# Latent attention with three-pass fp32r scores and a division after the context, written out without loops

## The chip, the cores and the metric

One core of one Trainium2 chip runs a whole model of two blocks in one program. The metric is device time in microseconds (us), the median over several executions. The names of the engines are those of the profile: PE is the TensorE matmul, PEld its weight load, DVE is VectorE, ACT is ScalarE, POOL is GpSimd, SP issues the DMAs.

## The reference

The input is 1024 tokens of 256 channels. Eight residual layers follow each other: an attention, an expert layer (64 experts), a second attention, the expert layer again, a third attention, a small feed-forward, a **latent attention**, and the small feed-forward again. The change is in the latent attention alone:

```python
bs, seq_len, _ = x.shape                       # 1, 1024
qc = rms_norm(x @ wq_down, q_norm_w)           # 96 channels
q_nope = (qc @ wq_up).reshape(bs, seq_len, H, DN)    # H = 16, DN = 128
q_pe = (qc @ wq_rope).reshape(bs, seq_len, H, DR)    # DR = 64
kvc = rms_norm(x @ wkv_down, kv_norm_w)        # 64 channels
kv = (kvc @ wkv_up).reshape(bs, seq_len, H, DN + DV)
k_nope, v = (kv[..., :DN], kv[..., DN:])
k_rope = (x @ wk_rope).reshape(bs, seq_len, 1, DR)
q_pe = apply_rope(q_pe, cos, sin)
k_rope = apply_rope(k_rope, cos, sin)
...
scores = jnp.einsum('bqhd,bkhd->bhqk', q, k) * scale
mask = jnp.triu(jnp.full((seq_len, seq_len), -jnp.inf, jnp.float32), k=1)
probs = jax.nn.softmax(scores.astype(jnp.float32) + mask, axis=-1).astype(q.dtype)
out = jnp.einsum('bhqk,bkhd->bqhd', probs, v).reshape(bs, seq_len, H * DV)
return out @ wo
```

## The kernel before

Each layer is a function that opens one or more blocks. In a block every engine has its own list of instructions, and semaphores order them; between two blocks all engines meet. The latent attention, `latent` (L1295), has four blocks after a layer norm.

`latent_down` (L1334) projects the tokens to 96 query, 64 key-value and 64 rope channels (`lat`), normalizes, ropes the key part and turns the result: `qcT` (96 x 1024) and `kT` (128 x 1024: 64 latent rows, 64 rope rows). Its DMAs, and those of the next two blocks, are issued on SP in the block of the layer norm (`load`, L1320).

`latent_weights` (L1429) folds the up projections: per head a 96 x 64 matrix that takes a query straight to the key latents (into `wq`, L1492), and one that takes the latent context to the output (`wvo`).

`latent_attend` (L1497) is the long one. Heads go in 8 **pairs** `i`. A pair takes 8 **steps** `t`, one for each tile of 128 queries; since the mask is causal, step t has t + 1 tiles of keys. A step does, for both heads a = 0, 1:

- `score` (L1567): q against kT in fp32 into two banks of PSUM for each head (L1577), and the mask added by a bf16 matmul (L1579);
- `maximum` on DVE (L1737), `exponentiate` on ACT (L1650), which also sums the row;
- `scale` on DVE: reciprocal of the sum (L1745), then the probabilities times it (L1748);
- `transposes` on PE (L1589) in groups of up to four key tiles, `copy_turned` on ACT (L1658) for both heads, `values` (L1599), which adds into one bank, `pv`, for four query tiles; `store` on DVE (L1753) moves that bank to `ctxT` after steps 3 and 7.

PE works one step behind itself: in step t it computes the scores of t, and then the transposes and values of t - 1 (`back`). Between them it projects a piece of the queries of the next half or the next pair (`project`, L1562 and L1564); `rotate` on DVE (L1732) and an add on POOL (L1705) rope it, and ACT copies the latent rows (L1642). Steps 1 to 4 thus handle values of tiles 0 to 3. The first and the last pair are written out; the six between are one loop on every engine (`Fori`). The order of all this is that of the code:

```python
for t in range(TT):
    for a in range(2):
        score(i, t, a)
    ...
        back(*((i, t - 1) if t else (i - 1, TT - 1)), between=next_part)
```

`latent_out` (L1777) multiplies `ctxT` by `wvo` and adds to the stream.

## Time and profile before

| | us |
|---|---|
| median of 3 runs | 2221.38 (2218.03 to 2227.26) |
| the profiled execution | 2218.32 |
| its span | 2216.3 |
| PE busy | 1916.7 (86% of the span) |
| DVE busy | 1164.1 (53%) |
| ACT busy | 912.3 (41%) |
| POOL busy | 597.5 (27%) |
| mean granted clock of PE | 0.911 |

The span is what the profiler saw between the first and the last instruction. Busy time of PE is modelled: matmuls overlap, so a length in a row is longer than the distance between two starts. The clock is given as a share of full speed; 1.00 is 2.4 GHz and 0.50 is 1.2 GHz.

### The profile page before, as it was taken

The numbers are of one execution on the slowest core, as the hardware profiler recorded it, in microseconds if no ns is written. First come the engines' busy times: TensorE is split into PE (matmuls) and PEld (weight loads), VectorE is DVE, ScalarE is ACT, GpSimd is POOL, SyncE is SP. The second block draws the span as 40 slices with busy tenths as digits, with TensorE's granted clock in tenths as the row PEclk, the third lists the DMA queues.
The fourth block names the chain that finished last, engine by engine and source line by source line (L and its number), as shares of the span: only waits on it lengthen the run. The fifth ranks groups of instructions, "written<-read, shape, count | busy, mean of one in ns | idle before, by whom it ended". The sixth has DMA issues, their size and how long they took to land. (4 is left out here: it accounts for less than half of the span.)

```text
span 2216.3 us, 30788 instructions
## 1 busy us (share of the span) xinstructions
PE 1916.7 (86%) x10273; PEld 1241.9 (56%) x10273; DVE 1164.1 (53%) x2032; ACT 912.3 (41%) x1932; POOL 597.5 (27%) x488
## 2 busy tenths in 40 slices
PE   4499689999998498699999985499976899999997
PEld 3133467888885265587888863033344455555566
DVE  4476334444444354344444456488833467777743
ACT  1177433333333265333333332087751045555531
POOL 1000246656662100456656534000000011111100
PEclk8599789999999699799999997599997599999998
DMA  2700153444430700444444401900004000000000
GB/s 75 107 1 1 38 131 102 112 123 106 106 85 0 108 2 24 97 123 115 106 103 106 126 3 51 135 8 1 1 1 102 0 1 1 0 0 0 0 1 20
DMA packets 128262, 123.11 MB, mean 56 GB/s; under 512 B 81448, under 2 KB 108208, under 8 KB 128016
## 3 DMA queue, kind: packets, MB, share of 16 engines
q1 hardware_dynamic: 128176, 121.99, 24.5%
q8 instruction: 51, 0.84, 0.2%
q14 instruction: 35, 0.29, 0.1%
HBM read 113.30 MB, written 8.65 MB: 55 GB/s over the span
## 5 line engine op out<-in xcount | busy, mean ns | idle before, releaser
L667 DVE TENSOR_TENSOR e_inner_lo<-e_inner_b,e_inner_hi 128x512 fp32r<-128x512 f32 x192 | 251.5, 1310 | 391.6 <-ACT e_inner_hi L614 391.6
L647 POOL TENSOR_TENSOR e_wsilu<-e_silu_b,e_rw 128x512 f32<-128x512 f32 x192 | 262.0, 1365 | 212.0 <-ACT e_silu_b L621 158.6
L554 PE MATMUL psum<-e_x_hi,e_w_hi 128*128 128x512 f32 x768 | 305.6, 398 | 5.8 <-DVE e_inner_b L678 4.4
L554 PE MATMUL psum<-e_x_lo,e_w_hi 128*128 128x512 f32 x768 | 301.1, 392 | 0.0
L554 PE MATMUL psum<-e_x_hi,e_w_lo 128*128 128x512 f32 x768 | 301.0, 392 | 0.0
L621 ACT ACTIVATE e_silu_b<-psum 128x512 f32<-128x512 f32 x192 | 114.7, 597 | 365.2 <-PE psum L554 365.2
L655 POOL TENSOR_TENSOR e_w_lo<-e_w_raw,e_w_hi 128x384 fp32r<-128x384 f32 x180 | 215.4, 1197 | 134.2 <-ACT e_w_hi L608 112.8
L1202 DVE TENSOR_REDUCE c_mx<-psum 128x1 f32<-128x1024 f32 x128 | 151.4, 1220 | 63.4 <-PE psum L1079 63.4
L554 PEld LDWEIGHTS psum<-e_x_hi,e_w_hi 128*128 128x128 f32 x768 | 145.6, 190 | 48.3 <-DVE e_inner_b L678 18.3
L1650 ACT ACTIVATE la_probs<-psum,la_negmax 128x256 f32<-128x256 f32 (+7 forms) x128 | 96.2, 752 | 175.9 <-DVE la_negmax L1737 175.9
L554 PEld LDWEIGHTS psum<-e_x_hi,e_w_lo 128*128 128x128 f32 x768 | 145.5, 189 | 31.0
L554 PEld LDWEIGHTS psum<-e_x_lo,e_w_hi 128*128 128x128 f32 x768 | 145.8, 190 | 29.7
L678 DVE TENSOR_TENSOR e_inner_b<-psum,e_wsilu 128x512 f32<-128x512 f32 x192 | 130.5, 680 | 58.8 <-POOL e_wsilu L647 58.8
L568 PE MATMUL psum<-e_inner_hi,e_w_hi 128*128 128x512 f32 x384 | 152.2, 396 | 4.1 <-DVE e_inner_lo L667 4.1
L1577 PE MATMUL psum<-l_kT,la_q 128*128 128x512 f32 (+3 forms) x384 | 150.9, 518 | 2.5 <-POOL la_q L1705 1.6
L1170 ACT ACTIVATE c_probs<-psum 128x512 f32<-128x512 f32 x256 | 138.5, 600 | 33.9 <-PE psum L1111 31.2
L568 PE MATMUL psum<-e_inner_hi,e_w_lo 128*128 128x512 f32 x384 | 149.7, 390 | 0.0
L568 PE MATMUL psum<-e_inner_lo,e_w_hi 128*128 128x512 f32 x384 | 149.6, 390 | 0.0
L608 ACT CAST e_w_hi<-e_w_raw 128x384 fp32r<-128x384 f32 x180 | 92.4, 513 | 122.0 <-PE psum L568 122.0
L614 ACT CAST e_inner_hi<-e_inner_b 128x512 fp32r<-128x512 f32 x192 | 117.7, 613 | 32.0 <-PE psum L568 16.9
L1737 DVE TENSOR_REDUCE la_negmax<-psum 128x1 f32<-128x256 f32 (+7 forms) x128 | 96.2, 757 | 58.7 <-PE psum L1579 57.1
L1705 POOL TENSOR_TENSOR la_q<-la_q,la_swapped 64x512 f32<-64x512 f32 x32 | 40.5, 1265 | 297.7 <-DVE la_swapped L1732 297.7
(303 smaller groups left out, 3116.9 us busy)
## 6 DMA issues: line engine op xcount, KB each, us to landing
e_rw<-e_rw_dram SPq DMA_DIRECT2D x64, 384.0 KB, 5.8
e_rw<-e_rw_dram SPq DMA_DIRECT2D x64, 256.0 KB, 5.4
e_w_raw<-in_L_ffn_w_gate SPq DMA_DIRECT2D x64, 192.0 KB, 2.6
e_w_raw<-in_L_ffn_w_up SPq DMA_DIRECT2D x64, 192.0 KB, 2.6
e_w_raw<-in_L_ffn_w_down SPq DMA_DIRECT2D x32, 384.0 KB, 3.5
e_rw<-e_rw_dram SPq DMA_DIRECT2D x64, 128.0 KB, 5.3
a_qs<-a_parts_dram SPq DMA_DIRECT2D x12, 256.0 KB, 9.3
b_qs<-b_parts_dram SPq DMA_DIRECT2D x12, 256.0 KB, 9.4
```

The source lines that it names most:

```text
L554: last = nc.tensor.matmul(bank[u % 2][:], parts.up_or_gate(a, s, which, k, j), parts.x[b][:, k, h * HALF:(h + 1) * HALF], start=(n == 0), ...
L568: last = nc.tensor.matmul(obank[2 * h + m][:], parts.down(a, s, j, m), inner_parts[b][:, u % 3, :], start=False, stop=False, skip_group_ch ...
L614: nc.scalar.copy(inner_parts[0][:, u % 3, :], inner[:, u % 2, :]).then_inc(high_made, 1)
L621: nc.scalar.activation(silu[:, u % 2, :], gbank[u % 2][:], ACT.Silu).then_inc(silu_done, 1)
L647: nc.gpsimd.tensor_tensor(wsilu[:, u % 2, :], silu[:, u % 2, :], rw[:, s, j, h * HALF:(h + 1) * HALF], ALU.mult).then_inc(weighted, 1)
L655: nc.gpsimd.tensor_tensor(parts.w[1][:, 1 - s, p, :], parts.raw[:, p, :], parts.w[0][:, 1 - s, p, :], ALU.subtract).then_inc(parts.low_mad ...
L667: nc.vector.tensor_tensor(inner_parts[1][:, u % 3, :], inner[:, u % 2, :], inner_parts[0][:, u % 3, :], ALU.subtract).then_inc(low_made, 1)
L678: nc.vector.tensor_tensor(inner[:, u % 2, :], ubank[u % 2][:], wsilu[:, u % 2, :], ALU.mult).then_inc(inner_ready, 1)
L1170: nc.scalar.activation(probs[:, step_of[p, j] % 2, x, 0:nq], ring_bank(("scores", p, j, x))[:, 0:nq], ACT.Exp, scale=HD ** -0.5).then_inc( ...
L1202: nc.vector.tensor_reduce(mx[:, p % 2, t % QUART, x:x + 1], max_buffer(n)[:, 0:cfg.max_width(t)], AX_X, ALU.max).then_inc(max_done, 1)
L1577: nc.tensor.matmul(out[:, k0:k0 + nk], q[:, a, t * P:(t + 1) * P], kT[:, k0:k0 + nk], start=True, stop=False, skip_group_check=True)
L1650: nc.scalar.activation(probs[:, a, t % 2, 0:w], scores_of(a)[:, 0:w], ACT.Exp, bias=negmax[:, a:a + 1], accum_out=sums[:, a, t % 2:t % 2 + ...
```

## The change

It rewrites the latent attention and leaves every other layer as it is.

- **Three passes.** Key, compressed query, query weights and query are each split into a high part and the rest, both fp32r. A product is three fp32r matmuls (high x high, high x low, low x high) instead of one in fp32. A score matmul is at least 256 columns wide; the columns past the causal edge are computed and never read.
- **Two heads in one projection.** One projection now serves both heads of a pair for 512 tokens: part 0 gives the latent rows of both, parts 1 and 2 the plain and the swapped rope rows. The key is stored twice, the second time with its halves exchanged, so that the second head has its rows the other way up. `latent_down` turns one more tile for each token tile and makes high and low copies; `latent_weights` does the same for `wq`.
- **The sums.** `scale` is gone. Once in four steps `invert` takes the reciprocal of the 8 sums (4 tiles, 2 heads), each written 64 times; PE turns the result (`inverse`), ACT copies it (`copy_inverse`), and `store` multiplies the context by it.
- **Who copies.** The turned probabilities of head 0 are now copied by DVE, those of head 1 by ACT. The two banks for turned tiles are used in turn by all groups and by `inverse`.
- **Order.** PE does score(0), the first transposes of both heads of the step before, score(1), and then the rest. All 8 pairs are written out.
- **Memory.** The rope tables for queries live in `core.xi` and now cover all 128 partitions (four DMAs instead of two), `probsT` lives in `core.xn`, the raw weights are given up before `latent_attend`.

```diff
+            wq = [sbi(n, [QR, 3, LPAIRS, P]) for n in ("wq_hi", "wq_lo")]
+            qc = [sbi(n, [QR, T]) for n in ("qc_hi", "qc_lo")]
+            kT = [sbi(n, [P, 2, T]) for n in ("kT_hi", "kT_lo")]
...
+            cos, sin = (core.xi[:, h:h + TT // 2, :].rearrange("p t d -> p (t d)") for h in (0, TT // 2))
...
+                    sp.dma_start(wkv[:], core.dram["L1_attn_b_wkv_up"]).then_inc(up_loaded, 16)
+                    sp.dma_start(wr[:], core.dram["L1_attn_b_wq_rope"].rearrange("r (h d) -> r h d", d=DR)).then_inc(up_loaded, 16)
+                    sp.dma_start(wo[:], core.dram["L1_attn_b_wo"].rearrange("(h p) n -> p h n", p=P)).then_inc(up_loaded, 16)
+                    for rows in (slice(0, DR), slice(DR, P)):
+                        sp.dma_start(cos[rows, :], core.dram["c_cos_q"]).then_inc(tab_loaded, 16)
+                        sp.dma_start(sin[rows, :], core.dram["c_sin_q"]).then_inc(tab_loaded, 16)
...
+                    nc.tensor.transpose(core.bank[4 + h][0:QR, span], lat[:, t, 0:QR], core.ident[:])
+                    nc.tensor.transpose(core.bank[6 + h][:, span], lat[:, t, QR:W], core.ident[:])
+                    last = nc.tensor.transpose(core.bank[h][:, span], lat[:, t, QR + KVR:W + KVR], core.ident[:])
...
-                nc.scalar.copy(kT[:, h * HALF:(h + 1) * HALF], core.bank[6 + h][:]).then_inc(qk_copied, 1)
+                span = slice(h * HALF, (h + 1) * HALF)
+                nc.scalar.copy(kT[0][:, 0, span], core.bank[6 + h][:]).then_inc(high_made, 1)
+                nc.scalar.copy(qc[0][:, span], core.bank[4 + h][0:QR, :]).then_inc(high_made, 1)
+                nc.scalar.copy(kT[0][:, 1, span], core.bank[h][:]).then_inc(high_made, 1)
...
+            nc.vector.tensor_copy(lat[:, :, W:W + KVR], lat[:, :, QR:QR + KVR]).then_inc(valued, 1)
...
+                dve.wait_ge(high_made, 3 * h + 1)
+                nc.vector.tensor_tensor(kT[1][:, 0, span], core.bank[6 + h][:], kT[0][:, 0, span], ALU.subtract).then_inc(low_made, 1)
...
+            for h in range(HEADS):
+                cols = slice(KVR * (h % 2), KVR * (h % 2) + KVR)
+                act.wait_ge(folded, h + 1)
+                nc.scalar.copy(wq[0][:, 0, h // 2, cols], core.bank[2 + h % 2][0:QR, 0:KVR]).then_inc(fold_high, 1)
...
+        whole = sb("q_whole", [P, 2, HALF])
+        rope, swap = sb("rope", [P, HALF]), sb("swap", [P, HALF])
...
+        inv_rows = sb("inv_rows", [P, HALF])
...
+            def project(m, part):
...
-                    last = nc.tensor.matmul(core.bank[7][KVR:P, :], wh[:, a, KVR + DR:KVR + 2 * DR], rhs, start=True, stop=True)
+                    pe.wait_ge(lat_copied, 2 * m + 2)
+                elif m or part:
+                    pe.wait_ge(roped, 2 * m + part // 2)
+                for n, (x, y) in enumerate(PASSES):
+                    last = nc.tensor.matmul(proj[:], wq[x][:, part, i, :], qc[y][:, half * HALF:(half + 1) * HALF],
+                                            start=n == 0, stop=n == len(PASSES) - 1)
                 last.then_inc(proj_ready, 1)
 
...
                 out = scores_of(a)
-                for k0 in range(0, (t + 1) * P, HALF):
-                    nk = min(HALF, (t + 1) * P - k0)
-                    nc.tensor.matmul(out[:, k0:k0 + nk], q[:, a, t * P:(t + 1) * P], kT[:, k0:k0 + nk],
-                                     start=True, stop=False, skip_group_check=True)
+                for x, y in PASSES:
+                    for k0 in range(0, (t + 1) * P, HALF):
+                        nk = max(min(HALF, (t + 1) * P - k0), WIDE)
+                        nc.tensor.matmul(out[:, k0:k0 + nk], q[x][:, i % 2, a, t * P:(t + 1) * P], kT[y][:, a, k0:k0 + nk],
+                                         start=(x, y) == PASSES[0], stop=False, skip_group_check=True)
...
+            def bank_free(key):
+                if turns[key] >= 2:
+                    pe.wait_ge(bank_copied[turns[key] % 2], turns[key] // 2)
+
+            def transposes(i, t, g, a):
+                if g == 0:
+                    pe.wait_ge(exp_done, n_unit(i, t, a) + 1)
+                bank_free((i, t, g, a))
+                for x, k in enumerate(groups[t][g]):
+                    last = nc.tensor.transpose(turn_bank((i, t, g, a))[:, x * P:(x + 1) * P],
+                                               probs[:, a, t % 2, k * P:(k + 1) * P], core.ident[:])
...
+            def inverse(i, half):
+                key = ("inverse", i, half)
+                pe.wait_ge(inverted, 2 * i + half + 1)
+                bank_free(key)
+                for t in range(HT):
+                    last = nc.tensor.transpose(turn_bank(key)[:, t * P:(t + 1) * P],
+                                               inv[:, half, t, :, :].rearrange("p a n -> p (a n)"), core.ident[:])
...
+                    n = turns[i, t, g, a]
+                    pe.wait_ge(bank_copied[n % 2], n // 2 + 1)
...
+            def rest(i, t, between=None):
+                for g in range(1, len(groups[t])):
+                    for a in range(2):
+                        transposes(i, t, g, a)
+                if t % HT == HT - 1:
+                    inverse(i, t // HT)
                 if between is not None:
-                    between()
-                for g in range(1, len(groups[t])):
-                    transposes(i, t, g)
+                    project(*between)
                 for g in range(len(groups[t])):
                     values(i, t, g)
...
+            former = None
+            for i, t in steps:
+                score(i, t, 0)
+                if former:
                     for a in range(2):
-                        score(i, t, a)
-
-                    def next_part():
-                        if projects(t, final):
-                            n, part, a, half = part_of(i, t)
-                            project(n, part, a, half, placed=2 * i + 3 + a if t >= HT and part == 0 else None)
-
-                    if early(i, t, 1):
-                        next_part()
-                    else:
-                        back(*((i, t - 1) if t else (i - 1, TT - 1)), between=next_part)
-
-            for n, part, a, half in FIRST:
-                project(n, part, a, half, placed=a + 1 if part == 0 else None)
-            pair(0)
-            with pe.Fori(1, LPAIRS - 1) as i:
-                pair(i)
-            pair(LPAIRS - 1, final=True)
-            back(LPAIRS - 1, TT - 1)
+                        transposes(*former, 0, a)
+                score(i, t, 1)
+                if former:
+                    rest(*former, between=part_at(i, t))
+                elif part_at(i, t):
+                    project(*part_at(i, t))
+                former = i, t
...
+            def copy_latent(m):
+                act.wait_ge(proj_ready, 3 * m + 1)
+                if m >= 1:
+                    act.wait_ge(q_ready, m)
+                for a in range(2):
+                    rows = slice(KVR * a, KVR * a + KVR)
+                    nc.scalar.activation(whole[rows, a, :], proj[rows, :], ACT.Copy, scale=LSCALE).then_inc(lat_copied, 1)
...
+            def copy_inverse(i, half):
+                key = ("inverse", i, half)
+                act.wait_ge(turned, turns[key] + 1)
+                if (i, half) != (0, 0):
+                    act.wait_ge(ctx_copied, 2 * i + half)
+                nc.scalar.copy(inv_rows[:], turn_bank(key)).then_inc(bank_copied[turns[key] % 2], 1)
...
+            for i, t in steps:
+                if former:
+                    copy_turned(*former, 0)
+                exponentiate(i, t, 0)
+                if former:
+                    for g in range(1, len(groups[former[1]])):
+                        copy_turned(*former, g)
+                    if former[1] % HT == HT - 1:
+                        copy_inverse(former[0], former[1] // HT)
+                exponentiate(i, t, 1)
+                if part_at(i, t) and part_at(i, t)[1] == 0:
+                    copy_latent(part_at(i, t)[0])
+                former = i, t
...
+                    nc.gpsimd.tensor_tensor(whole[rows, a, :], rope[rows, :], swap[rows, :], ALU.add).then_inc(summed, 1)
+                pool.wait_ge(summed, 2 * m + 2)
+                pool.wait_ge(lat_copied, 2 * m + 2)
+                if m >= 4:
+                    pool.wait_ge(score_ready, n_unit(m // 2 - 1, 0, 0))
+                nc.gpsimd.tensor_copy(q[0][:, buf, :, span], whole[:]).then_inc(split, 1)
+                pool.wait_ge(split, m + 1)
+                nc.gpsimd.tensor_tensor(q[1][:, buf, :, span], whole[:], q[0][:, buf, :, span], ALU.subtract).then_inc(q_ready, 1)
...
+            def rotate(m, part):
+                dve.wait_ge(proj_ready, 3 * m + part + 1)
+                if m >= 1 and part == 1:
+                    dve.wait_ge(summed, 2 * m)
+                out, table = (rope, cos) if part == 1 else (swap, sin)
+                nc.vector.scalar_tensor_tensor(out=out[:], in0=proj[:], scalar=LSCALE,
+                                               in1=table[:, m % 2 * HALF:(m % 2 + 1) * HALF],
+                                               op0=ALU.mult, op1=ALU.mult).then_inc(roped, 1)
...
+            def copy_turned(i, t, g):
+                key, n = (i, t, g, 0), len(groups[t][g]) * P
+                dve.wait_ge(turned, turns[key] + 1)
+                if values_of[i, t, g] >= 2:
+                    dve.wait_ge(pv_done, values_of[i, t, g] - 1)
+                nc.vector.tensor_copy(probsT[:, group_buffer(i, t, g), 0, 0:n],
+                                      turn_bank(key)[:, 0:n]).then_inc(bank_copied[turns[key] % 2], 1)
+
+            def invert(i, half):
+                dve.wait_ge(exp_done, n_unit(i, HT * half + HT - 1, 1) + 1)
+                if i >= 1:
+                    dve.wait_ge(turned, turns["inverse", i - 1, half] + 1)
+                nc.vector.reciprocal(inv[:, half, :, :, :],
+                                     sums[:, half, :, :].unsqueeze(3).broadcast_to([P, HT, 2, KVR])).then_inc(inverted, 1)
...
+                dve.wait_ge(pv_done, values_of[i, t, len(groups[t]) - 1] + 1)
+                dve.wait_ge(bank_copied[turns[key] % 2], turns[key] // 2 + 1)
+                nc.vector.tensor_tensor(ctxT[:, i, half * HALF:(half + 1) * HALF], pv[:], inv_rows[:],
+                                        ALU.mult).then_inc(ctx_copied, 1)
...
+            former = None
+            for i, t in steps:
+                maximum(i, t, 0)
+                if former:
+                    if former[1] % HT == HT - 1:
+                        invert(former[0], former[1] // HT)
+                    copy_turned(*former, 0)
+                maximum(i, t, 1)
+                if former:
+                    back(former, part_at(i, t))
+                elif part_at(i, t) and part_at(i, t)[1] > 0:
+                    rotate(*part_at(i, t))
+                former = i, t
+            invert(former[0], 1)
+            copy_turned(*former, 0)
+            back(former)
```

**Order on DVE, step 4 of a pair.** `la_` names the tiles of `latent_attend`; `xn` is now `probsT`. Before:

```order
L1737 TENSOR_REDUCE la_negmax<-psum 128x1 x2
L1745 RECIPROCAL la_inv<-la_sums 128x1
L1748 TENSOR_SCALAR la_probs<-la_probs,la_inv 128x640
L1732 SCALAR_TENSOR_TENSOR la_q<-psum,l_cos 64x512
L1745 RECIPROCAL la_inv<-la_sums 128x1
L1748 TENSOR_SCALAR la_probs<-la_probs,la_inv 128x640
L1753 TENSOR_SCALAR l_ctxT<-psum 128x512
```

Now, from the second maximum of step 3 and the first of step 4 (one row):

```order
L1769 TENSOR_REDUCE la_negmax<-psum 128x1 x2
L1784 RECIPROCAL la_inv<-la_sums 128x512
L1777 COPY xn<-psum 128x512
L1769 TENSOR_REDUCE la_negmax<-psum 128x1
L1792 TENSOR_TENSOR l_ctxT<-psum,la_inv_rows 128x512
```

The reciprocal of 512 elements stands behind the first maximum of the step, and ahead of the copy of the turned tiles and of the second maximum.

**Order on PE, the same step.** Before:

```order
L1577 MATMUL psum<-l_kT,la_q 128x512
L1577 MATMUL psum<-l_kT,la_q 128x128
L1579 MATMUL psum<-mh_prev,ident_h 128x128
L1589 MATMUL psum<-ident,la_probs 128x128 x8
L1562 MATMUL psum<-l_qcT,la_wh 128x512
L1599 MATMUL psum<-la_probsT,l_v 64x128 x8
```

Now, from the transposes between the two heads' scores:

```order
L1623 MATMUL psum<-ident,la_probs 128x128 x8
L1609 MATMUL psum<-l_kT_hi,la_q_hi 128x512
L1609 MATMUL psum<-l_kT_hi,la_q_hi 128x256
L1609 MATMUL psum<-l_kT_lo,la_q_hi 128x512
L1609 MATMUL psum<-l_kT_lo,la_q_hi 128x256
L1609 MATMUL psum<-l_kT_hi,la_q_lo 128x512
L1609 MATMUL psum<-l_kT_hi,la_q_lo 128x256
L1611 MATMUL psum<-mh_prev,ident_h 128x128
L1632 MATMUL psum<-ident,la_inv 128x128 x4
L1596 MATMUL psum<-l_qc_hi,l_wq_hi 128x512
L1596 MATMUL psum<-l_qc_lo,l_wq_hi 128x512
L1596 MATMUL psum<-l_qc_hi,l_wq_lo 128x512
```

The four transposes of `la_inv` stand between the second head's scores and the projection; the values come after both.

## Rows read from the trace of the kernel before

**Rows 1.** Windows: start us to end us, length, each engine's busy us, clock, DMA.

```profile
1764.50:1775.40 10.90, 7.96 (x8) 1.58 (x8) 2.08 (x3) 2.46 (x3) 1.95 (x3) 0.50 0.00 1
1849.10:1894.40 45.30, 43.87 (x301) 26.33 (x297) 33.10 (x59) 23.35 (x62) 5.74 (x6) 1.00 0.00 0
```

**Rows 2.** Timeline of PE: start us, length us, line, operation, tiles, shape, count.

```profile
1902.91 1.98 PE L1577 MATMUL psum<-l_kT,la_q 128*128 128x512 f32 x4
...
1906.62 1.04 PE L1589 MATMUL psum<-ident,la_probs 128*128 128x128 f32 x8
...
1911.22 0.49 PE L1577 MATMUL psum<-l_kT,la_q 128*128 128x128 f32 x2
...
1912.81 1.02 PE L1562 MATMUL psum<-l_qcT,la_wh 96*128 96x512 f32 x2
1913.67 1.04 PE L1589 MATMUL psum<-ident,la_probs 128*128 128x128 f32 x8
1914.64 2.00 PE L1599 MATMUL psum<-la_probsT,l_v 128*64 128x128 f32 x32
1916.57 0.70 PE L1577 MATMUL psum<-l_kT,la_q 128*128 128x256 f32 x2
...
1928.39 1.35 PE L1577 MATMUL psum<-l_kT,la_q 128*128 128x512 f32 x4
```

**Rows 3.** Timeline of PE in an expert stage, fp32r matmuls.

```profile
1214.13 0.39 PE L554 MATMUL psum<-e_x_lo,e_w_hi 128*128 128x512 f32 x1
...
1218.21 0.39 PE L554 MATMUL psum<-e_x_lo,e_w_hi 128*128 128x512 f32 x1
```

**Rows 4.** Timeline of PE, fp32 matmuls of 8 moving columns.

```profile
1657.17 5.28 PE L243 MATMUL psum<-wrt,xT 128*128 128x8 f32 x32 [1.03 <-PEq L162]
```

**Rows 5.** Groups by form on DVE: count | busy us, mean ns | idle before.

```profile
L1745 DVE RECIPROCAL la_inv<-la_sums 128x1 f32<-128x1 f32 x128 | 20.7, 161 | 13.3 <-ACT la_probs L1650 10.6
...
L199 DVE COPY xT<-psum 128x512 f32<-128x512 f32 x16 | 11.0, 687 | 6.2 <-PE psum L216 6.2
...
L1229 DVE RECIPROCAL a_rden<-psum 128x16 f32<-128x16 f32 x8 | 2.1, 258 | 27.3 <-PE psum L1138 27.3
...
L183 DVE RECIPROCAL n_rstd_b<-n_std_b 128x8 f32<-128x8 f32 x8 | 1.6, 203 | 2.2 <-ACT n_std_b L204 2.2
```

**Rows 6.** Groups by form, last stages: the largest and a middle maximum, the latent copy.

```profile
L1642 ACT ACTIVATE la_q<-psum 64x512 f32<-64x512 f32 x32 | 18.8, 587 | 47.2 <-PE psum L1562 47.2
L1737 DVE TENSOR_REDUCE la_negmax<-psum 128x1 f32<-128x1024 f32 x16 | 19.6, 1224 | 26.6 <-PE psum L1579 26.6
...
L1737 DVE TENSOR_REDUCE la_negmax<-psum 128x1 f32<-128x640 f32 x16 | 13.2, 824 | 3.1 <-PE psum L1579 2.8
```

**Rows 7.** Groups by form on POOL.

```profile
L1705 POOL TENSOR_TENSOR la_q<-la_q,la_swapped 64x512 f32<-64x512 f32 x32 | 40.5, 1265 | 297.7 <-DVE la_swapped L1732 297.7
...
L435 POOL TENSOR_TENSOR e_x_lo<-xT,e_x_hi 128x1024 fp32r<-128x1024 f32 x4 | 9.6, 2396 | 351.7 <-ACT e_x_hi L421 351.5
```

**Rows 8.** Windows at the start of the first expert stage.

```profile
290.30:293.70 3.40, 1.20 (x6) 0.66 (x5) 0.69 (x1) 0.71 (x2) 2.06 (x2) 1.00 1.04 248
293.70:297.10 3.40, 3.40 (x8) 2.67 (x9) 2.06 (x2) 0.92 (x2) 2.79 (x3) 0.50 1.03 239
```

**Rows 9.** Timeline of PE there: in brackets idle us before, and what ended it.

```profile
293.61 0.74 PE L554 MATMUL psum<-e_x_hi,e_w_hi 128*128 128x512 f32 x1 [2.20 <-DVE e_inner_b L678]
```

**Rows 10.** Timeline of PE in the third attention.

```profile
1373.38 0.87 PE L871 MATMUL psum<-ident,c_qk 128*128 128x128 f32 x6 [2.35 <-DVE c_qk L923]
```

**Rows 11.** Timeline of SP's queue before the latent down projection.

```profile
1692.63 12.91 SPq L1325 DMA_DIRECT2D l_cos<-in_c_cos_q  x1
...
1705.58 0.60 SPq L1326 DMA_DIRECT2D l_sin<-in_c_sin_q  x1
```

**Rows 12.** Timeline of POOL in the attention: one add of successive pairs.

```profile
2056.00 1.26 POOL L1705 TENSOR_TENSOR la_q<-la_q,la_swapped 64x512 f32<-64x512 f32 x1 [9.02 <-DVE la_swapped L1732]
...
2101.30 1.26 POOL L1705 TENSOR_TENSOR la_q<-la_q,la_swapped 64x512 f32<-64x512 f32 x1 [8.99 <-DVE la_swapped L1732]
```

More of the change, by code:

```diff
@@ new lines, in back @@
+            def back(former, between=None):
+                i, t = former
+                for g in range(1, len(groups[t])):
+                    copy_turned(i, t, g)
+                if between and between[1] > 0:
+                    rotate(*between)
+                if t % HT == HT - 1:
+                    store(i, t // HT)
+            dve.wait_ge(tab_loaded, 64)
+            for m in range(2):
+                for part in (1, 2):
+                    rotate(m, part)
+            former = None
```

332 lines of the change are left out of this document (128 added, 204 removed).

## The prediction

> **What bounds the kernel now.** I read the page first, for where the latent attention lies (its lines begin at about 1687 us of the 2216.3 us span), then windows, to see which engine fills it. From the second pair on, a pair takes 45.3 us, of which PE is busy 43.9, DVE 33.1, ACT 23.4 and POOL 5.7, at full clock [rows 1]: PE sets the pace. The timeline of PE says how. In step 7 nothing waits: 8.31 us from its first score matmul (1902.91) to that of the next step (1911.22), of which the two heads' scores take 3.71 [rows 2]. Steps 1 to 3 (1916.57 to 1928.39) take 11.8 us for little work [rows 2]; there PE waits for the chain maximum, exponential, reciprocal, scaling, transposes, copy.
>
> From starts in rows 2: the last 8 transposes, 0.97 us, some 0.11 each without their waits; a projection 0.86; a value matmul (1.93 / 32) 0.060. A pair has 16 units of scores (17.8 us, added up from their starts; the 3.71 us of step 7 stand for them), 8 projections (6.9), 72 transposes (7.9) and 144 value instructions (8.7), together 41.3 us. So **4.0 of the 45.3 us are waits**.
>
> **The change, PE's work.** Eighteen fp32r matmuls of 512 columns lie between the two rows of an expert stage, 4.08 us, 0.227 each [rows 3]. Scores of step 7: 12 of them and two masks (0.07 each), 2.86 us instead of 3.71. For 256 columns no row stands. The lower end is half of 0.227, 0.11; the upper is 0.227 itself, if short ones gain nothing. 32 matmuls of 8 columns, with full weight loads, started 5.28 / 32 = 0.165 us apart, partly at half clock [rows 4]; I take 0.13, nearer to the lower end, since that row bounds the load from above. The 16 units are then 14.4 us a pair (steps 0 to 7, one head: 0.45, 0.45, 0.59, 0.75, 1.13, 1.13, 1.27, 1.43). Projections: 6 x 3 x 0.227 = 4.1. Transposes: 72 and 8 of the reciprocals, 8.8. Values as before, 8.7. Sum **36.0 us, 5.3 less**.
>
> **The change, waits.** Scaling leaves the chain, and the copies are shared by DVE and ACT. I walked through steps 1, 2, 3, 5, 6 and 7 with the durations of the rows: all but 0.5 us of waits go. But `invert` is new. A reciprocal took 161 ns for 1 element a row, 203 for 8, 258 for 16 [rows 5]: 6.5 ns for each further element. 512 elements, most of them copies of 8 sums, make 258 + 496 x 6.5 = **3.5 us**. The lower end is what DVE takes for an ordinary copy of 512, 0.69 [rows 5]; the upper is 4.3, at 8 ns an element. The slope is the same between all three sizes, so I take 3.5.
>
> The Trainium skill, VectorE: DVE Perf Modes, "Walkthrough: the 8-slice pipeline in each mode", says that reciprocal is an iterated divide with a repeat count of 8. Eight repeats of 1.04 ns, the step of an ordinary element, would be an estimate of 4.4 us instead of 3.5, and 14 us more in all.
>
> Where it stands decides. *Step 4:* scores of head 0 are over after 1.3 us; the maximum of 640 takes 0.82 [rows 6] (2.15), `invert` 3.5 (5.65), the copy 0.69 (6.35). PE has done its transposes and the second head's scores at 3.1. Its next instructions, the transposes of `la_inv`, need both `invert` and the bank that DVE has not copied. PE idles **3.2 us**. *Step 0* is the same with the values of step 7: the maximum (0.29 for 128, at 1.04 ns an element below the 1.22 for 1024 [rows 6]) is over at 0.94, `invert` at 4.4, the copy at 5.1; PE idles from 1.8, 3.3 us, and 0.5 us more when the transposes of `la_inv` wait for the second copy. Behind `invert` are also the second maximum and the exponential; both are done again before step 5 or 1 needs them. Waits: 3.8 + 3.2 + 0.5 = 7.5 us. **A pair takes 43.5 us, 1.8 less; eight, 14 us less.** ACT then has some 24 us a pair and POOL 2 x 6.2 (below), both under cover.
>
> **The change, outside the pairs.**
> - *The start.* Before, 10.9 us at half clock [rows 1]. Now project, ACT's two copies (2 x 0.59) [rows 6], project and rotate twice: some 7.4 us for m = 0. `copy_latent` of m = 1 needs POOL to be done with `whole`: two adds of 1.27, a copy of some 1.2 (estimate: half the next), a subtraction of 2.40 [rows 7], 6.2 us; then another five before the first score. About 18.5, so **+8**. The small steps behind it are also at half clock, with less work to raise it: **+3**.
> - *`latent_down`.* Eight more transposes at half clock (0.22 each), one more DVE copy in front (0.42), three ACT copies in a row instead of one (1.2), a subtraction behind the last (0.6): **+3.9**.
> - *DMAs.* SP's first rope-table issue held it 12.9 us, its second 0.60 [rows 11], and `latent_down` begins when SP is through. Two more issues: 1.2 us, from 0.6 to some 10 if the queue is full again. I take **+1.2**, since the second found room at once.
> - *`latent_weights`.* ACT's high copy comes into DVE's chain (0.2 us a head), which has slack against PE there; POOL's twelve operations lie beside the folds. Nothing; if the slack is gone, 16 x 0.3.
> - *The end.* The last pair's tail has `invert`, but no step behind it: **-2** against the sum above.
> - *No loops.* POOL's adds in the looped and in the written-out last pair are 45.30 us apart [rows 12], against 45.3 a pair in the loop: nothing either way.
>
> 2218.3 - 14 + 8 + 3 + 3.9 + 1.2 - 2 = 2218.4 us: by work alone, no change.
>
> **The clock.** Twice a pair PE now idles over 3 us. At the start of an expert stage PE idled 2.20 us for DVE [rows 9]; in that window PE was busy 1.20 of 3.40 us, and the granted clock of the next 3.4 us was 0.50, though PE was busy throughout [rows 8]. A gap of 2.35 us in the third attention [rows 10] had no fall. So gaps of 3.2 to 3.3 us should nearly always be followed by a stretch at half clock. One costs up to half of 3.4 us, 1.7, as PE is the bound right behind it: 15 gaps (7 in step 0, 8 in step 4) make **+26**, between 0 and 51 (two such stretches each). Sum 2244.4 us against the profiled 2218.3; that execution lies 3.1 us below the median of the runs, so I predict **2248 us**.
>
> **The rivals.**
> 1. *The reciprocal is cheap* (0.7 us at 512: a start-up cost explains the slope of small sizes). The two waits shrink by 2.8 each, no clock falls: 2218.4 - 8 x 5.6 = 2173.6, on the median's scale 2177: faster. For it: no row has more than 16 elements. Against: the slope is the same from 1 to 8 and from 8 to 16. It decides below about 1.8 us. Chance 0.10; with it, that my walk counts too little overlap elsewhere (2200), 0.08.
> 2. *The clock holds* through the gaps: 2218.4 + 3.1, no change. For it: the gap of 2.35 us. Against: rows 8 and 9. 0.14.
> 3. *Eight full repeats an element*, 4.4 us: 15 gaps longer by 0.9, 2262. For it: only that the slope of 6.5 ns is nearer to 8 than to 1; against: the slope itself. The rule is the one of the skill's page above. 0.10.
> 4. *Half clock for long*: behind a fall the short steps 1 to 3 don't raise it, and two stretches follow each gap: 2273. The 10.9 us before the first score ran at half clock with PE busy 8.0 of them [rows 1]. 0.06.
> 5. *Short fp32r matmuls gain nothing*: 24 a pair cost 0.1 more, +19 us. It moves any case up; a bound, not a case of its own.
>
> **How the numbers follow.** Forecast 0.52 (about 2232 to 2265), rivals as above. The range has to leave out no more than 2 in 10: rival 1 with its cheap reciprocal (0.10), part of its second half and of rival 4 beyond 2278 go. That gives 2207 to 2278. 0.5% is 11 us, about what a measurement of this kernel can tell from no change. Slower: the forecast but for its lower edge (0.46), rivals 3 and 4: 0.62. No change: rival 2 and that edge: 0.20. Faster: 0.18.
>
> **What would show it.** The reciprocal's row: 3.5 us, 16 of them. Windows of a pair: 43 to 46 us, PE busy some 38 of them, granted clock below 1.00, about 0.85. Timeline: PE idle 3 us before the first transposes of a second group (step 0) and before those of `la_inv` (step 4), released by DVE. Score matmuls of fp32r 0.227 us apart at full clock. The first score 18 us after the first projection. Wrong if the reciprocal takes under 2 us, if the clock is 1.00 through the pairs, or if a pair takes less than 42 us.

## The result, and the profile after

| us | before | changed |
|---|---|---|
| median of 4 runs each, one chip | 2220.24 (2218.03 to 2227.26) | 2258.56 (2253.21 to 2265.92) |
| profiled execution, its span | 2218.32, 2216.3 | 2265.92, 2264.1 |
| first projection to `latent_out` | 377.5 | 412.3 |
| mean granted clock of PE | 0.911 | 0.892 |

The ratio is 1.0171, 95% interval 1.0151 to 1.0190: slower by 1.7%, 38 us. The forecast was 2248, in a range that holds the result. The two profiled spans differ by 47.8 us; 6.8 of that lie in the layers ahead of the latent attention, which the change does not touch, so the stages are compared one by one. The profiled execution of the changed kernel is the slowest of its four.

Windows of the changed kernel (columns as in [rows 1]): an ordinary pair, and in it two stretches at step 0 of the next pair.

```profile
1844.79:1892.68 47.89, 42.08 (x333) 32.89 (x331) 27.89 (x36) 21.47 (x50) 11.94 (x8) 0.93 0.01 1
1894.52:1897.93 3.41, 0.52 (x5) 0.39 (x5) 3.17 (x3) 0.71 (x3) 0.00 (x0) 1.00 0.01 2
1897.93:1901.34 3.41, 3.39 (x14) 2.46 (x12) 0.69 (x1) 1.53 (x4) 0.00 (x0) 0.50 0.02 5
```

A pair took 45.3 us at full clock before [rows 1] and takes 47.9 now, with PE busy 42.1 (partly at half clock). The second and third rows are one event: PE busy 0.52 of 3.41 us, DVE busy 3.17, and then 3.41 us at clock 0.50 (the level of 1.2 GHz), although PE was busy throughout. DVE's timeline and PE's say what it is.

```profile
1893.40 0.29 DVE L1769 TENSOR_REDUCE la_negmax<-psum 128x1 f32<-128x128 f32 x1 [1.59 <-PE psum L1611]
1893.61 3.34 DVE L1784 RECIPROCAL la_inv<-la_sums 128x512 f32<-128x512 f32 x1
1896.87 0.63 DVE L1777 COPY xn<-psum 128x512 f32<-128x512 f32 x1
```

```profile
1894.44 0.23 PE L1611 MATMUL psum<-mh_prev,ident_h 128*128 128x128 bf16 x1
1897.56 1.66 PE L1623 MATMUL psum<-ident,la_probs 128*128 128x128 f32 x8 [2.89 <-DVE xn L1777]
...
1918.33 1.03 PE L1632 MATMUL psum<-ident,la_inv 128*128 128x128 f32 x4 [2.82 <-DVE xn L1777]
```

The reciprocal holds DVE 3.34 us, the bank's copy stands behind it, and PE idles 2.89 us before the transposes of a second group (step 0) and 2.82 before those of `la_inv` (step 4). Behind each of the 16 gaps there is a stretch at half clock, 14 times one of 3.4 us and twice one of 6.8. The group's row has one length for all (count | busy us, mean ns | idle before):

```profile
L1784 DVE RECIPROCAL la_inv<-la_sums 128x512 f32<-128x512 f32 x16 | 53.5, 3344 | 0.8 <-ACT la_probs L1696 0.8
```

### The profile page after: what moved, and what is told of

Same layout as the page of the kernel before. It is cut to its first block and busy times, and to the rows that moved or that the text cites. A ratio compares the mean times of both kernels' runs of the same rounds, so it can differ in the third digit from the quotient of the medians.

```text
span 2264.1 us, 30190 instructions
## 1 busy us (share of the span) xinstructions
PE 1914.4 (85%) x10542; PEld 1310.0 (58%) x10553; DVE 1126.8 (50%) x1861; ACT 902.2 (40%) x1872; POOL 653.2 (29%) x513
## 5 line engine op out<-in xcount | busy, mean ns | idle before, releaser
L1746 POOL TENSOR_TENSOR la_q_whole<-la_rope,la_swap 64x512 f32<-64x512 f32 x32 | 40.8, 1276 | 286.0 <-DVE la_swap L1762 284.8
L1079 PE MATMUL psum<-c_ks,c_qs 96*128 96x512 bf16 x256 | 86.4, 423 | 38.2 <-DMA c_ks<-c_parts_dram 35.2
L1202 DVE TENSOR_REDUCE a_mx<-psum 128x1 f32<-128x128 f32 (+7 forms) x128 | 91.1, 753 | 49.9 <-PE psum L1079 49.0
```

Of the source, the lines that this page charges most:

```text
L1202: nc.vector.tensor_reduce(mx[:, p % 2, t % QUART, x:x + 1], max_buffer(n)[:, 0:cfg.max_width(t)], AX_X, ALU.max).then_inc(max_done, 1)
```

## The experiments

The theory: the long reciprocal, where it stands, makes both gaps, and each gap brings a stretch at half clock. e1 to e4 test it; e5 to e8 and e11 price single parts on top of e1; e9, e10 and e12 look for the best version. Each time stands beside runs of the kernel before on the same chip.

**e1, the reciprocal of 8 sums and a copy.**

```diff
-nc.vector.reciprocal(inv[:, half, :, :, :],
-                     sums[:, half, :, :].unsqueeze(3).broadcast_to([P, HT, 2, KVR])).then_inc(inverted, 1)
+nc.vector.reciprocal(one[:, half, :, :], sums[:, half, :, :]).then_inc(one_made, 1)
+dve.wait_ge(one_made, 2 * i + half + 1)
+nc.vector.tensor_copy(inv[:, half, :, :, :],
+                      one[:, half, :, :].unsqueeze(3).broadcast_to([P, HT, 2, KVR])).then_inc(inverted, 1)
```

> The changed kernel with the reciprocal taken of the 8 sums alone (about 0.2 us) and spread over the 64 places each by an ordinary copy (0.69 us at most, as the 128x512 copy); all results as before. Theory (the 3.34 us of the long reciprocal make both gaps, and each gap makes the half-clock stretch behind it): the gaps shrink from 2.85 us to some 0.4, so 16 x 2.5 = 40 us go, and 16 stretches of 3.4 us at half clock go, 1.7 each = 27 us: 2258.6 - 67 = about 2191 us, a pair about 43.5 us, granted clock 1.00 inside the pairs. Rival A (the clock falls for another reason, and stays low behind these places): 2218 us, clock still about 0.93 in a pair. Rival B (something else, the bank's copy or the other engine, ends the wait as late as before): over 2240 us, gaps still over 2 us.

Measured: 2198.64 us (before 2218.60), ratio 0.9907, 0.9885 to 0.9929. Windows, the second pair:

```profile
1835.47:1876.21 40.74, 39.04 (x333) 30.66 (x331) 23.31 (x38) 21.32 (x50) 11.94 (x8) 1.00 0.01 1
```

The gaps are 0.25, 0.44 and 0.91 us, the clock 1.00. Rivals A and B fall. The gain is 60 us, not the 67 expected: where one wait a pair stood at 2.89 us two of together 0.69 stand now, and 0.91 stands for 2.82, so the waits give 4.1 us a pair and not 5. (The expected pair of 43.5 us did not fit its own sum: 47.9 less 5.0 of waits and 3.4 of clock would be 39.5.) One expression made the change 60 us slower than it need be, and turned a gain of 0.9% into a loss of 1.7%.

**e2, the gaps filled.** At the head of `rest`, in steps 0 and 4:

```diff
+if t % HT == HT - 1 and (between is not None or i + 1 == LPAIRS):
+    m = between[0] if between else 2 * LPAIRS
+    pe.wait_ge(roped, 2 * m)
+    for _ in range(11):
+        nc.tensor.matmul(proj[:], wq[0][:, 0, 0, :], qc[0][:, 0:HALF], start=True, stop=True)
```

> The changed kernel, the long reciprocal and its place kept, but PE runs 11 superfluous fp32r matmuls of 512 columns (0.227 us each, 2.5 us) into the idle projection bank just where it would wait; nothing of the computation is changed. Theory (the half-clock stretches follow from PE's idle time, and PE is the bound behind them): waiting time is the same, the gaps seen on PE shrink to about 0.3 us, no fall of the clock, 2258.6 - 16 x 1.7 = about 2231 us. Rival A (work behind a fall isn't bound by PE's clock, so that it costs nothing): 2258 us with the clock at 1.00. Rival B (the clock falls at these places whatever PE does): granted clock unchanged, and at half clock the 11 matmuls take up to 5 us: over 2265 us.

Measured: 2236.52 us (before 2218.60), ratio 1.0073, 1.0049 to 1.0096. Windows, the second pair, and PE in its step 0:

```profile
1840.28:1885.53 45.25, 44.21 (x354) 34.45 (x352) 27.90 (x36) 21.32 (x50) 11.93 (x8) 1.00 0.00 1
```

```profile
1842.08 2.79 PE L1654 MATMUL psum<-l_qc_hi,l_wq_hi 96*128 96x512 f32 x11
1845.15 1.09 PE L1623 MATMUL psum<-ident,la_probs 128*128 128x128 f32 x8 [0.29 <-DVE xn L1782]
1846.69 0.63 PE L1632 MATMUL psum<-ident,la_inv 128*128 128x128 f32 x4 [0.44 <-DVE xn L1782]
```

PE waits as long for DVE as before (3.07 us from 1842.08 on), but it is busy, and no stretch at half clock follows. Useless work saved 22 us by the medians; from first projection to `latent_out` it is 412.3 against 385.9, 26 us. That is the clock's price alone, 22 to 26 us (27 expected); rivals A and B fall.

**e3, the long reciprocal twice.**

```diff
+nc.vector.reciprocal(inv[:, half, :, :, :],
+                     sums[:, half, :, :].unsqueeze(3).broadcast_to([P, HT, 2, KVR])).then_inc(once, 1)
+dve.wait_ge(once, 2 * i + half + 1)
 nc.vector.reciprocal(inv[:, half, :, :, :],
...
```

> The changed kernel with the long reciprocal made twice in a row, the second over the first's result. Theory (DVE's reciprocal is on the path with its whole length at both places): 16 x 3.36 = 54 us more, 2312 us, the gaps 6.2 us each; the clock's stretches at half speed are partly used up in the gap itself, so they cost between 27 us less and 14 us more than now: 2285 to 2326 us. Rival (other work takes up part of it, as PE has slack later in the pair): less than 27 us more, below 2285.

Measured: 2313.18 us (before 2218.60), ratio 1.0426, 1.0400 to 1.0452. That is 54.6 us over the changed kernel: 16 x 3.36 = 54. PE's timeline:

```profile
1931.38 1.09 PE L1633 MATMUL psum<-ident,la_inv 128*128 128x128 f32 x4 [6.21 <-DVE xn L1778]
```

Nothing takes up any of it. The stretch at half clock is now 6.8 us, but half of it lies in the gap, so it costs neither more nor less than with the short gaps.

**e4, the long reciprocal later in the queues.** On ACT `copy_inverse` also goes behind the second exponential.

```diff
 maximum(i, t, 0)
 if former:
-    if former[1] % HT == HT - 1:
-        invert(former[0], former[1] // HT)
     copy_turned(*former, 0)
...
 for g in range(1, len(groups[t])):
     copy_turned(i, t, g)
+if t % HT == HT - 1:
+    invert(i, t // HT)
...
-if t % HT == HT - 1:
-    inverse(i, t // HT)
 if between is not None:
     project(*between)
 for g in range(len(groups[t])):
     values(i, t, g)
+if t % HT == HT - 1:
+    inverse(i, t // HT)
```

> The changed kernel with the same long reciprocal, but placed later in three queues: on DVE behind the copies and the second head's maximum of its step, on PE its transposes behind the projection and the values, on ACT its copy behind the second exponential. Theory (what costs is where it stands, in front of a copy that PE needs): the wait before a group's transposes goes; PE reaches the transposes of the reciprocals 3.5 us after the start of the rest in step 0 and 2.4 in step 4, DVE is through at about 4.8 and 4.2, so waits of 1.3 and 1.8 us stay, below the 2.85 of now by 1.3 on average: 16 x 1.3 = 21 us, and no fall of the clock, 27 us: about 2211 us. Rival (DVE is late anyway, and the next step's maximum waits in its place): within 10 us of the changed kernel's 2258.6, with a new gap before a score or a first group's transposes.

Measured: 2232.49 us (before 2218.60), ratio 1.0060, 1.0038 to 1.0082. It saves 26 us, not 48. PE in step 4 of the third pair, and the windows of its wait and of what follows:

```profile
1899.10 1.12 PE L1632 MATMUL psum<-ident,la_inv 128*128 128x128 f32 x4 [2.40 <-DVE la_inv L1784]
```

```profile
1896.70:1899.10 2.40, 0.00 (x1) 0.01 (x1) 2.34 (x1) 0.00 (x1) 0.00 (x0) 1.00 0.03 7
1899.12:1902.53 3.41, 3.41 (x14) 2.91 (x15) 0.92 (x2) 1.66 (x3) 0.00 (x0) 0.50 0.00 0
```

In step 0 a wait of 1.0 us is left and the clock stays up; in step 4 it is 2.40 us (expected 1.8), and the clock falls behind it. Place matters, but a moved 3.34 us is still late where little other work stands.

**e5, the start** (on e1). `part_at` gives pair 0 its own table; PE's and DVE's heads shrink to the first half.

```diff
+if i == 0:
+    return ((1, 1), (1, 2), (2, 0), (2, 1), (2, 2), (3, 0), (3, 1), (3, 2))[t]
...
-for m in range(2):
-    for part in range(3):
-        project(m, part)
+for m, part in ((0, 0), (0, 1), (0, 2), (1, 0)):
+    project(m, part)
```

> e1 with the projections of the first pair's second half, and those of the second pair, spread over the steps 0 to 7 of the first pair, so that the first scores stand right behind the first half's q and not behind the second half's; the same work. Theory (the start's 19.2 us from first projection to first score, and the later gap of 3.3 to 4.4 us in step 1, come from score(0) standing behind projections that wait for POOL to give `whole` free): the first score comes 5 us earlier, and most of the gap of step 1 goes, 7 to 9 us in all: 2198.6 - 8 = about 2190 us. Rival (POOL's own 6.2 us a half bind the first pair in either order): gaps of the same sum elsewhere in the first pair, 2196 us or more.

Measured: 2189.98 us (before 2221.83), ratio 0.9870, 0.9845 to 0.9895; 8.7 us under e1. The first score comes 14.1 us behind the first projection, not 19.2. That is the whole gain between first projection and `latent_out` (344.8 us in e5, 349.9 in e1): from the first score on both take 330.7. The shorter wait of step 1 (2.40 us for 4.37) is paid back by the second pair (41.5 us for 40.7), so for that part the rival holds. The medians, which come from two chips, make the gain 3.6 us larger than these two traces do. The changed kernel's wait there, which the new order removes:

```profile
1793.29 0.79 PE L1596 MATMUL psum<-l_qc_hi,l_wq_hi 96*128 96x512 f32 x1 [5.85 <-ACT la_q_whole L1687]
```

**e6, the tables later** (on e1). The four rope-table DMAs leave `load` for a function `tables`, which `latent_down` gets as `load_later`.

```diff
 norm(load)
 block = ctx.enter_context(nc.Block())

+@block.sync
+def _(sp):
+    load_later(sp)
```

> e1 with the four rope-table DMAs issued in the block of latent_down and no more in that of the norm ahead of it. Theory (SP's 13.6 us issue ends the norm's block, and nothing else there is late; PE turned the norm's output by 1702.8 of a start of 1715.9): latent_down starts 12 us earlier, 2198.6 - 12 = about 2187 us. Rival (the weights of latent_down are themselves late, or the tables then hold up latent_attend): 2193 us or more.

Measured: 2186.49 us (before 2221.83), ratio 0.9846, 0.9830 to 0.9863; 12.2 us under e1. SP's queue in the changed kernel, then SP and PE in e6:

```profile
1699.65 13.62 SPq L1330 DMA_DIRECT2D xi<-in_c_cos_q  x1
```

```profile
1698.22 8.49 SPq L1332 DMA_DIRECT2D xi<-in_c_cos_q  x1
```

```profile
1693.56 3.67 PE L216 MATMUL psum<-ident,xn 128*128 128x128 f32 x16 [6.58 <-DVE xn L187]
1698.26 3.98 PE L1380 MATMUL psum<-ld_w,xT 128*128 128x224 f32 x10 [1.03 <-PEq L162]
```

The issue still stalls, but `latent_down` no longer waits for it: it starts 4.7 us behind the norm's first transpose, not 16.5 as in e1.

**e7, the mask between the passes** (on e1).

```diff
 for x, y in PASSES:
+    if (x, y) == PASSES[1]:
+        nc.tensor.matmul(out[:, t * P:(t + 1) * P], core.ident_h[:], core.mask_h["prev"][:, 1, :],
+                         start=False, stop=False, skip_group_check=True)
...
-nc.tensor.matmul(out[:, t * P:(t + 1) * P], core.ident_h[:], core.mask_h["prev"][:, 1, :],
-                 start=False, stop=True, skip_group_check=True).then_inc(score_ready, 1)
+last.then_inc(score_ready, 1)
```

> e1 with the mask's matmul of each of the 128 score units between the first and the second fp32r pass, not behind the third; the same work. Theory (what lengthens each step by 0.2 to 0.4 us over the forecast is a price of some 0.1 us for the first fp32r matmul behind one of another type): one more such change in each unit, 128 x 0.1 = 13 us: about 2211 us, a pair 42.4 us instead of 40.8. Rival (the first matmul is late because its weights load behind a short matmul or behind a semaphore, whatever the type): the mask in between costs nothing, 2198.6 within 3 us.

Measured: 2201.17 us (before 2221.83), ratio 0.9908, 0.9891 to 0.9924; 2.5 us over e1, a pair 41.2. PE, one unit of e1 and the same of e7:

```profile
1883.17 0.39 PE L1610 MATMUL psum<-l_kT_hi,la_q_hi 128*128 128x256 f32 x1
1883.39 0.28 PE L1610 MATMUL psum<-l_kT_lo,la_q_hi 128*128 128x256 f32 x1
1883.51 0.29 PE L1610 MATMUL psum<-l_kT_hi,la_q_lo 128*128 128x256 f32 x1
1883.64 0.23 PE L1612 MATMUL psum<-mh_prev,ident_h 128*128 128x128 bf16 x1
1883.70 0.39 PE L1624 MATMUL psum<-ident,la_probs 128*128 128x128 f32 x2
```

```profile
1888.19 0.39 PE L1613 MATMUL psum<-l_kT_hi,la_q_hi 128*128 128x256 f32 x1
1888.42 0.23 PE L1609 MATMUL psum<-mh_prev,ident_h 128*128 128x128 bf16 x1
1888.46 0.36 PE L1613 MATMUL psum<-l_kT_lo,la_q_hi 128*128 128x256 f32 x1
1888.66 0.28 PE L1613 MATMUL psum<-l_kT_hi,la_q_lo 128*128 128x256 f32 x1
1888.78 0.38 PE L1626 MATMUL psum<-ident,la_probs 128*128 128x128 f32 x2
```

A pass of 256 columns takes 0.12 us from start to start, the first one 0.22. In e7 the second pass, now behind the mask, takes 0.20 too: so the first fp32r matmul behind another type does cost 0.08 to 0.10 more. But the mask gets shorter by 0.02, and a projection right behind a third pass loses its own surcharge (0.24 instead of 0.31): a unit goes from 0.53 to 0.59 us, and the expected 13 us is 3. The time lies within the rival's 3 us, but the rows decide against the rival's reason: the surcharge is real. It is the theory's size that is wrong, since a switch more costs 0.06 net.

**e8, scores in one fp32 pass** (on e1).

```diff
-for x, y in PASSES:
-...
+nc.tensor.matmul(out[:, k0:k0 + nk], q[0][:, i % 2, a, t * P:(t + 1) * P].bitcast(F32),
+                 kT[0][:, a, k0:k0 + nk].bitcast(F32), start=True, stop=False, skip_group_check=True)
```

> e1 with the scores in one fp32 pass over the high parts alone, as wide as needed (the low parts of q and k are left out of the scores; they are still made). Theory (the three fp32r passes are what shortens PE's work, 17.8 us a pair against 14.4 and 16 changes of type of 0.1): a pair 1.8 us longer, 40.8 to 42.6, 8 x 1.8 = 14 us: about 2213 us. Rival A (no cost of the change of type): 3.4 us a pair, 2226 us. Rival B (three passes bring nothing over fp32, and e1's gain is all from the scaling that left the chain): 2198.6 within 4 us.

Measured: 2211.86 us (before 2221.83), ratio 0.9951, 0.9934 to 0.9968; 13.2 us over e1. Windows, the second pair:

```profile
1839.40:1881.86 42.46, 40.98 (x308) 27.82 (x306) 23.01 (x38) 21.43 (x50) 11.83 (x8) 1.00 0.01 1
```

The three passes are worth 1.7 us a pair, as expected. Rivals A and B fall.

**e11, the projection in one fp32 pass** (on e1).

```diff
-for n, (x, y) in enumerate(PASSES):
-...
+nc.tensor.matmul(proj[:], wq[0][:, part, i, :].bitcast(F32), qc[0][:, half * HALF:(half + 1) * HALF].bitcast(F32),
+                 start=True, stop=True).then_inc(proj_ready, 1)
```

> e1 with each projection as one fp32 matmul over the high parts alone (the low parts of the weights and of the latent are left out of the projection; they are still made). Theory (three fp32r passes take 0.87 us with the changes of type around them, as e1's timeline shows, 0.31, 0.23 and 0.33, and one fp32 pass 0.86 as before): the same time within 4 us of 2198.6, so the projections gained only by being 6 instead of 8. Rival (my forecast's size, 0.68 us for three passes): 48 x 0.17 = 8 us longer, 2207 us.

Measured: 2204.98 us (before 2220.84), ratio 0.9927, 0.9906 to 0.9948; 6.3 us over e1, a pair 41.7. The rival was nearer. A projection in three passes does take 0.87 us, but one in fp32 with the values behind it takes 1.01, not the 0.86 that stood before other work:

```profile
1889.38 1.08 PE L1596 MATMUL psum<-l_qc_hi,l_wq_hi 96*128 96x512 f32 x2
1890.39 0.44 PE L1643 MATMUL psum<-xn,l_v 128*64 128x128 f32 x4
```

**e9 and e10, all together, the projections joined to the next scores.** The first diff is e9's, the second e10's (both against the changed kernel's order).

```diff
-if between is not None:
-    project(*between)
 for g in range(len(groups[t])):
     values(i, t, g)
+if between is not None:
+    project(*between)
```

```diff
 if t % HT == HT - 1:
+    if between is not None:
+        project(*between)
     inverse(i, t // HT)
-if between is not None:
-    project(*between)
 for g in range(len(groups[t])):
     values(i, t, g)
+if between is not None and t % HT < HT - 1:
+    project(*between)
```

> The short reciprocal of e1, the start of e5 and the tables of e6 in one kernel, and each projection put behind the values of its step, right ahead of the next step's scores, so that two changes of type in a row fall together; results as before. Theory (the three gains lie in different places and add: 8.6 and 12.1 us from e1's 2198.6 give 2178; the joined projection saves some 0.2 us each, 48 of them, 9 us): about 2169 us. Rival (a projection that comes late holds ACT's copy of it, and with it the next exponential, so that the joining costs what it saves): 2178 us or more.

> e9, but in steps 0 and 4 the projection stands ahead of the transposes of the reciprocals, where PE still waits 0.44 and 0.91 us for DVE's copy. Theory (it fills these waits): 7 x 1.35 = 9 us under e9 at best, less the 0.2 us that each of the 14 loses by not being joined (3 us): 6 us under e9, about 2163 us. Rival (PE's waits there are only moved to the value matmuls behind ACT's copy): within 2 us of e9.

Measured: e9 2196.09 us, 0.9883 (0.9860 to 0.9905); e10 2186.21 us, 0.9833 (0.9800 to 0.9866), both with before at 2220.84. Both are over 20 us above their forecasts, 2169 and 2163. A pair of e9 takes 42.5 us, against e1's 40.7: the rival's time holds for e9, though not its reason, since no wait of PE in these pairs is put down to ACT. DVE and POOL in its step 4:

```profile
1883.53 1.97 DVE L1794 COPY la_inv<-la_one 128x512 f32<-128x512 f32 x1
1885.42 0.68 DVE L1785 COPY xn<-psum 128x512 f32<-128x512 f32 x1
```

```profile
1882.85 2.37 POOL L1761 TENSOR_TENSOR la_q_lo<-la_q_whole,la_q_hi 128x1024 fp32r<-128x1024 f32 x1
```

The late projection makes POOL's split late, and the split now lies on DVE's copy (more on it at the end): PE waits 1.71 us before `la_inv`, not 0.91, and 0.56 before values in step 1, where e1 has no wait. e10 takes 10 us back, more than the expected 6; its pair of 40.7 us is no shorter than e1's, and e12's, without the joining, is 39.5: the joining costs 1.2 us a pair.

**e12, the best version:** e1, e5 and e6, and in `rest`:

```diff
+if between is not None:
+    project(*between)
 if t % HT == HT - 1:
     inverse(i, t // HT)
-if between is not None:
-    project(*between)
```

> The short reciprocal of e1, the start of e5 and the tables of e6, with the projections ahead of the values as in the changed kernel, and in steps 0 and 4 also ahead of the transposes of the reciprocals (e10 without the joining); results as before. Theory (joining cost 1.7 us a pair in e9, since DVE's rotation of a late projection stands ahead of the next step's work; the three gains add, and the projection fills the waits of 0.44 and 0.91 us): 2198.6 - 8.6 - 12.1 = 2178, less 7 x 1.2 = 8: about 2170 us, a pair 39.6. Rival (the waits are only moved): 2178 us, a pair 40.8.

Measured: 2175.92 us (before 2220.93), ratio 0.9802, 0.9784 to 0.9820. Windows, a pair:

```profile
1857.10:1896.58 39.48, 38.96 (x333) 30.69 (x331) 23.32 (x38) 21.38 (x50) 11.96 (x8) 1.00 0.01 2
```

PE is busy 38.96 of 39.48 us. The pair is as the theory had it. The time is not: 2175.9 lies between its 2170 and the rival's 2178, and 3.5 of the 6 us missing are what e5 is worth less in the traces (5.1) than in the medians (8.6) that the sum used. e12 beats the kernel before by 2.0% and the changed one by some 83 us.

## Why the prediction came out as it did

- **The reciprocal**: 3.5 us forecast, 3.34 measured. From 16 elements (258 ns [rows 5]) to 512 (3344) a further one costs 6.2 ns. Rivals 1 and 3 fall. The estimate from the repeat count in the Trainium skill, VectorE: DVE Perf Modes, "Walkthrough: the 8-slice pipeline in each mode", is 4.4 us, which the measured 3.34 does not bear out.
- **The waits of `invert`**: 3.3 and 3.2 us forecast, 2.89 and 2.82 measured, at the places named. Right.
- **The clock**: 26 us forecast; e2 gives 26 in the attention and 22 by the medians. A gap costs somewhat less than 1.7 in an ordinary pair ((47.89 - 45.25) / 2 = 1.3), but there are 16 and not 15, since the last pair's end has one, and two are followed by 6.8 us at half clock. Rival 2 falls, and so does rival 4: behind 14 of the 16 there is one stretch. How long a wait PE can stand is not sharp: 2.35 us in the third attention had no fall [rows 10], 2.40 us in e4 had one, 1.0 us in e4 had none.
- **What a pair had to give**: the step that failed. Forecast 43.5 us without the clock, measured 45.25 (e2). The table adds up PE's rows of a pair, each from its start to the next one's less the wait shown in brackets; the 22 filling matmuls of e2 (5.6 us) count as waits. A short wait that lies under the modelled length of a row counts as work.

| us a pair | before, forecast's reading | before, rows | changed, forecast | e2, rows |
|---|---|---|---|---|
| scores and masks | 17.8 | 18.0 | 14.4 | 15.9 |
| projections | 6.9 | 7.6 | 4.1 | 5.2 |
| transposes | 7.9 | 9.0 | 8.8 | 8.2 |
| values | 8.7 | 9.4 | 8.7 | 9.4 |
| work | 41.3 | 44.0 | 36.0 | 38.7 |
| waits | 4.0 | 1.3 | 7.5 | 6.5 |

Without the clock a pair was to lose 9.3 us and to gain 7.5 of waits. It lost 6.6 and gained 6.5. The scores saved 2.1 us, not 3.4; the projections 2.3, not 2.8; transposes and old waits together 2.1, not 3.1. Two readings were wrong. The first is the pitch: 0.227 us came from a stage where fp32r follows fp32r [rows 3], and here one unit in three instructions begins with a surcharge of 0.1, so that a projection takes 0.87 us (e1's starts: 0.31, 0.23, 0.33) and not 0.68. The second is that "4.0 of the 45.3 us are waits", all but 0.5 of which would go. The rows show 1.3 us of waits before, and PE was busy 43.87 of 45.30 us in [rows 1]. Short waits can hide in the 72 transposes, which took 9.0 us before and take 7.4 in e2; that is 1.5 more at the most. The other 1.2 us are starts of groups, which the pitches from inside long runs left out, and they stay: the values take 9.4 us before and after. That the rows of work got 5.3 us shorter, just as forecast, is luck: too little in scores and projections, more in the transposes. Rival 5 falls: an fp32r matmul of 256 columns takes 0.12 us, near the 0.13 of the sum.

- **The last pair's end**: -2 against eight full pairs. From first score to `latent_out` e2 takes 366.7 us, 0.3 less than before. Eight full pairs make 0.7 of that and the start (next item) +2.6, so -2.2 are left: the end behind the eighth pair is 0.9 us longer than before, but the first pair has no step 0 with a wait in it. Right.
- **The start**: +8 forecast; 19.2 against 10.5 us, +8.7. Right. What follows it, +3: e1's first pair takes 43.2 us, later ones 40.8, and before the first was 0.2 shorter than the others, so +2.6. The size is right, but the half clock that the forecast named is not all of it. In step 1 PE also waits 3.28 us for ACT's copy, which the forecast did not have, and is at half clock for 6.8 us behind it; before, the half clock ended 6 us behind the first score and did not come back:

```profile
1805.66 0.72 PE L1596 MATMUL psum<-l_qc_hi,l_wq_hi 96*128 96x512 f32 x1 [3.28 <-ACT la_q_whole L1687]
```

```profile
1802.36:1805.77 3.41, 0.13 (x2) 0.11 (x2) 0.42 (x1) 1.32 (x3) 1.95 (x1) 1.00 0.00 0
1805.77:1812.60 6.83, 6.83 (x24) 4.39 (x26) 2.14 (x4) 2.67 (x10) 0.00 (x0) 0.50 0.01 2
```

- **`latent_down` and `latent_weights`**: +3.9 and 0; from first matmul to first projection 62.05 against 58.04, +4.0. Right.
- **SP**: +1.2; 17.5 against 15.3 us from the norm's first transpose to `latent_down`, +2.2. The two further issues took 0.60 each, and the stalled one 13.62 instead of 12.91 [rows 11].

So the long reciprocal, its place, the two waits and the clock's fall behind them were foreseen, and they are what makes the kernel slower. The forecast was 10 us low. From first projection to `latent_out`, without the clock, its sum was 5 us less than before (8 + 3 - 14 - 2), and e2 is 8.4 us more (385.9 against 377.5). These 13 us are the pairs: eight were to save 14 us and saved 0.7. By the medians the clock's 22 us for 26 take 4 of them back.

That the scaling left the chain is not what e8's pair, with fp32 scores, owes its 42.5 us to, against 45.3 before. By the same rows 2.3 of these 2.9 us are the six projections for eight; transposes and waits together take 10.3 us before and 10.2 in e8, since the transposes of the sums and the waits for them came in the scaling's place. The scaling was not taken out alone. That written-out loops cost nothing was not tried alone either.

## What to carry to other kernels

Take a reciprocal of the distinct values only and spread them with a copy; on a broadcast operand each copy is paid at 6 ns. Price a wait of the bound engine twice: its length, and the stretch at half clock behind it. Where the wait can't be removed, work put into it keeps the clock up even if it is useless (e2), and useful work gets the time itself back (e12's projection, 1.3 us a pair). A pitch read from a long run of like matmuls is too low for groups of three; read it where the types change. And before the rest of a sum is called waits, set it beside the idle time that the window shows: here 4.0 stood against 1.4.

## What was not expected

The broadcast copy of e1, 128x512 in SBUF, takes 0.43 us at step 0 and 1.18 at step 4. Timelines of DVE and POOL in e1:

```profile
1853.55 1.18 DVE L1787 COPY la_inv<-la_one 128x512 f32<-128x512 f32 x1
```

```profile
1852.06 2.38 POOL L1754 TENSOR_TENSOR la_q_lo<-la_q_whole,la_q_hi 128x1024 fp32r<-128x1024 f32 x1
```

POOL's subtraction ends at 1854.44, the copy 0.29 us later; in e9 POOL ends at 1885.22 and the copy of 1.97 us 0.28 later. By these rows the copy waits for POOL's instruction as a whole. The Trainium skill, SBUF — State Buffer, "SBUF: two separate sides", says that DVE and GpSimd share a port pair as "an **exclusive lock**, not a bandwidth split"; these rows agree. The last pair of e1 is the test: it has no projection of a next pair, so POOL does nothing there, and the copy of the same step 4 takes 0.43 us, where it took 1.17 or 1.18 in all seven pairs before it. PE's wait for `la_inv` falls with it, from 0.91 to 0.17 us.

```profile
2096.13 0.43 DVE L1787 COPY la_inv<-la_one 128x512 f32<-128x512 f32 x1
2097.30 0.63 PE L1633 MATMUL psum<-ident,la_inv 128*128 128x128 f32 x4 [0.17 <-DVE xn L1778]
```
